# Tower of four Fourier layers: a new order on VectorE in layer 0, and unread TensorE products in layers 0, 1 and 2

## What is computed

```
v = concat(x, gx, gy) @ p_w + p_b                      # one pixel value and two grid values lifted to 32 channels
for i in range(4):
    x_ft = rfft2(v)
    out1 = einsum('bixy,ioxy->boxy', x_ft[:, :, :12, :12],  W1[i])
    out2 = einsum('bixy,ioxy->boxy', x_ft[:, :, -12:, :12], W2[i])
    x1 = irfft2(place out1 and out2 in zeros)
    v = x1 + einsum('bcxy,cd->bdxy', v, w_w[i]) + w_b[i]
    v = batchnorm(v) ; if i < 3: v = relu(v)
out = einsum('bcxy,cu->bxyu', v, q_w) + q_b
```

## Time and profile before

| | |
|---|---|
| median of 3 runs | 760.6 us (759.24, 760.6, 770.03) |
| profiled execution | 765.84 us, span 763.9 us |
| PE busy | 630.4 us, 83% of the span, 10483 instructions |
| DVE busy | 543.5 us, 71% |
| ACT busy | 365.9 us, 48% |
| POOL busy | 51.2 us, 7% |
| mean granted clock of TensorE | 0.933 |
| layer 0 up to the end of mixing | 0 to 41.8 us |
| layer 1, forward transforms and mixing | 125.1 to 204.9 us |
| layer 2, forward transforms and mixing | 286.3 to 369.3 us |
| tower | up to about 577 us of 763.9 |

### The profile page before, as it was taken

The page is one execution under the profiler, slowest core; times in us unless marked ns, Lnnn a source line. Parts: engine busy times, 40 slices in busy tenths (PEclk is TensorE's granted clock), DMA queues, the critical chain, the costliest instruction groups (busy, mean ns, idle before and its releaser), DMA issues. The chain is left out here.

```text
span 763.9 us, 22872 instructions
## 1 busy us (share of the span) xinstructions
PE 630.4 (83%) x10483; PEld 417.0 (55%) x10483; DVE 543.5 (71%) x756; ACT 365.9 (48%) x533; POOL 51.2 (7%) x88
## 2 busy tenths in 40 slices
PE   3799964677799917777999849998998999999997
PEld 2777741234676612336767513344546787887744
DVE  6858886997479878984499858883613867657463
ACT  0015468800045659300155559754403777786762
POOL 4000000002000000001000000001001011111200
PEclk9999996999799969997599959999998999999999
DMA  8101100004012000013011000013104000000001
GB/s 329 27 22 44 44 2 1 1 1 147 3 44 60 6 1 1 1 43 106 6 60 44 2 1 2 2 43 106 30 3 155 2 2 2 1 2 2 1 1 28
DMA packets 11694, 26.31 MB, mean 34 GB/s; under 512 B 3408, under 2 KB 4176, under 8 KB 11600
## 3 DMA queue, kind: packets, MB, share of 16 engines
q1 hardware_dynamic: 11312, 24.21, 9.6%
q10 hardware_dynamic: 288, 0.66, 0.3%
HBM read 24.34 MB, written 0.52 MB: 33 GB/s over the span
## 5 line engine op out<-in xcount | busy, mean ns | idle before, releaser
L459 ACT ACTIVATE V<-ps,wts 128x1024 f32<-128x1024 f32 x96 | 101.8, 1111 | 241.9 <-PE ps L812 241.9
L633 DVE BATCH_NORM_STATS2 stats<-V 128x6 f32<-128x512 f32 x192 | 117.9, 676 | 16.1 <-ACT V L459 16.1
L509 DVE STREAM_TRANSPOSE room<-V 128x2048 f32<-128x2048 f32 x48 | 107.2, 2271 | 6.7 <-ACT V L408 6.7
L705 PE MATMUL ps<-room,tab 128*128 128x384 f32 x192 | 73.9, 523 | 31.1 <-DVE room L516 31.1
L408 ACT ACTIVATE V<-V,small 128x2048 f32<-128x2048 f32 x48 | 96.7, 2085 | 3.8 <-DVE small L660 3.8
L693 PE MATMUL ps<-room,tab 32*32 32x512 f32 x1536 | 67.6, 649 | 24.0 <-DVE room L509 24.0
L705 PEld LDWEIGHTS ps<-room,tab 128*128 128x128 f32 x192 | 35.3, 197 | 80.3 <-DVE room L516 57.3
L812 PEld LDWEIGHTS ps<-tab,room 64*128 64x128 f32 x1024 | 61.3, 192 | 29.6 <-issue 25.2
L627 DVE STREAM_TRANSPOSE room<-ps 128x2048 f32<-128x2048 f32 x24 | 55.6, 2317 | 22.0 <-PE ps L755 22.0
L516 DVE STREAM_TRANSPOSE room<-ps 128x1024 f32<-128x1024 f32 x48 | 56.6, 1217 | 19.4 <-PE ps L693 19.4
L812 PE MATMUL ps<-tab,room 64*128 64x128 f32 x1024 | 67.5, 283 | 1.8 <-DVE room L627 1.8
(11 more groups left out here) (230 smaller groups left out, 887.9 us busy)
## 6 DMA issues: line engine op xcount, KB each, us to landing
room<-in_modes SPq DMA_DIRECT2D x28, 384.0 KB, 5.8
r_ky<-in_modes SPq DMA_DIRECT2D x20, 384.0 KB, 3.1
wl<-in_layers SPq DMA_DIRECT2D x3, 452.0 KB, 5.8
wm<-in_mixture SPq DMA_DIRECT2D x1, 874.5 KB, 8.4
tab<-in_table SPq DMA_DIRECT2D x1, 656.5 KB, 4.8
room<-in_turned SPq DMA_DIRECT2D x1, 512.0 KB, 3.7
V<-in_pixels SPq DMA_DIRECT2D x4, 128.0 KB
out_dram<-ke SPq DMA_DIRECT2D x4, 128.0 KB, 2.5
```

Of the source, the lines that this page charges most:

```text
L459: nc.scalar.activation(Vm[:, 2 * h:2 * h + 2, r, 512 * q:512 * (q + 1)], bank(half_of_u(q, r) + 2 * h, 2).rearrange("p (m n) -> p m n", m= ...
L509: nc.vector.transpose(T[n % 3].rearrange("p (k n) -> p k n", k=16), Vk[:, :, P * n:P * (n + 1)]).then_inc(s_T, 1)
L633: last = nc.vector.bn_stats(stats[:, 16 * q + 4 * r + m, :], Vm[:, m, r, 512 * q:512 * (q + 1)])
L705: last = nc.tensor.matmul(bank(4 + (2 * (u % 2) if l < L - 1 else 0) + pair)[:, 0:MODES * CH], fwd_x[layout][ri], y[:, :, MODES * ri:MODES ...
```

## The change

Three edits. First, in layer 0 VectorE lifts two pairs ahead of the loop instead of three, and in the loop turns pair `k` before it lifts pair `k + 2`, where it lifted pair `k + 3` before it turned pair `k`. Second, TensorE gets unread products in layer 0: two of 512 columns ahead of mixing 0, and two of 256 columns behind each of the six mixing steps (behind the matmul that signals `s_mix`), into columns 256 to 511 of bank 7. Third, in layers 1 and 2 TensorE waits for the first relu of the layer and then issues three unread products of 512 columns ahead of the first `forward_y`. No transfer is added or moved.

```diff
--- before.py
+++ after.py
@@ -609,15 +609,15 @@
                     break
 
                 if l == 0:
-                    for k in range(3):
+                    for k in range(2):
                         lifted(k)
                 for k in range(KYP):
-                    if l == 0 and k + 3 < KYP:
-                        lifted(k + 3)
                     dve.wait_ge(s_mix, KYP * l + k + 1)
                     src = bank(2 * (k % 2), 2).rearrange("p (h j b) -> p b h j", h=2, b=BATCH)
                     dst = MZ[:, 1024 * k:1024 * (k + 1)].rearrange("p (b h j) -> p b h j", h=2, j=16)
                     nc.vector.transpose(dst, src).then_inc(s_Z, 1)
+                    if l == 0 and k + 2 < KYP:
+                        lifted(k + 2)
 
                 def spread_x(quad):
 
@@ -724,6 +724,10 @@
                     if l == L - 1:
                         for m in range(early):
                             convolve(m)
+                    else:
+                        pe.wait_ge(s_relu, PAIRS * (l - 1) + 1)
+                        for _ in range(3):
+                            nc.tensor.matmul(bank(7), first, tab[:, 0:512], start=True, stop=True)
                     forward_y(0)
                     for u in range(FU):
                         between = squares_in(u) if l == L - 1 else ()
@@ -740,6 +744,8 @@
                     pe.wait_ge(s_S, FU * l)
                 else:
                     pe.wait_ge(s_lyt, 2)
+                    for _ in range(2):
+                        nc.tensor.matmul(bank(7), first, tab[:, 0:512], start=True, stop=True)
 
                 def grid_of(quad):
 
@@ -779,6 +785,10 @@
                                 out = bank(2 * (k % 2) + kxh)[64 * par:64 * (par + 1), BATCH * kx:BATCH * (kx + 1)]
                                 last = nc.tensor.matmul(out.rearrange("p (i b) -> p i b", b=2),
                                                         W[ky][rows, kx, :], src, start=True, stop=True, tile_position=(64 * kxh, 64 * par))
+                    if l == 0:
+
+                        for _ in range(2):
+                            nc.tensor.matmul(bank(7)[:, 256:512], first, tab[:, 0:256], start=True, stop=True)
                     if l == L - 1:
 
                         convolve(late + k)
```

## The result

The changed kernel takes 752.5 us in the median of 20 runs (747.4 to 760.8), the kernel before 765.1 in 20 runs beside them (759.2 to 770.5). The ratio is 0.984, with a 95% interval from 0.982 to 0.987: 12 us, or 1.6%, faster, which is within the 2% that the prediction allowed on either side. The median of 760.6 that the prediction started from was that of three runs and turned out 4.5 us too low. So 752 predicted against 752.5 measured is partly luck: two errors cancel, a base 4.5 us too low and a gain of 8.6 us where this comparison shows 10 to 14. Two later comparisons of the same pair gave 0.989 (0.984 to 0.994) and 0.984 (0.980 to 0.987).

A forecast was written before the change was run, and what follows sets the result against it. It saw TensorE at 1.2 GHz in layer 0's mixing and VectorE setting the pace in layer 1's forward transforms. Gains of 6.0 us (layer 0) and 2.6 us (layers 1 and 2) off the 760.6 us median gave 752 us, range 747 to 761.5.

The forecast's parts named there:

- Layer 0: Layer 0: 4.0 us from mixing, 1.8 and 0.5 behind it; taken as 6.0 us, bounds -1.9 and 6.3.
- the rise in the first unread products: Layer 0: TensorE's clock rises between 15 and 20 us and stays up.
- rounds of 3.73 us: Layer 0: one turn and lift on VectorE takes 3.73 us and sets the pace of mixing.
- unread products hidden in TensorE's slack: Layer 0 mixing: a warm TensorE round of 2.9 us fits in VectorE's 3.73, with 0.8 us to spare.
- the last layer's row: Last layer: mixing sharing 3.65 us rounds with other products shows clock 1.00, taken as evidence that layer 0 stays warm.
- the cold order alone: Layer 0: with mixing still at 1.2 GHz, the new order gains 2.5 us if nothing else stands in line.
- Rival A: Layer 0: clock does not rise or hold, unread products queue; rounds 5.2 us, total 763.3 us; chance 0.13.
- second HAM failure mode: TensorE: brief idling between matmul groups lets the clock swing; by this rule Rival A would hold, at 763.3 us.
- The starts: Start of layers 1 and 2: three unread products speed the first y product; 1.3 us each, 2.6 together.
- The bound of 0.4 us for their delay: Start of layers 1 and 2: the three products, if cold, delay the first y product by at most 0.4 us.
- Rival B: Layer 0: warm mixing is not paced by its matmuls (1.28 us stall mid-block); rounds 4.4 us, total 755.4; chance 0.17.
- rival C: Layers 1 and 2: mid-layer clock falls shift, winning or losing 4 to 5 us (747.5 or 756.5); chance 0.10.

The follow-up runs named there:

- e1: The changed kernel without the three unread products at the start of layers 1 and 2; ratio to the kernel before 0.996 (0.993 to 0.999).
- e7: The changed kernel without the pairs of 256-column products behind layer 0's six mixing steps; ratio to the kernel before 0.990 (0.987 to 0.993).
- e4: The kernel before plus only layer 0's unread products, with the old order of lifts and turns; ratio to before 1.001 (0.996 to 1.006).
- e3: The kernel before plus only layer 0's new order of lifts and turns, no new unread products; ratio to before 1.002 (0.997 to 1.007).
- e5: The changed kernel plus two 256-column unread products behind each mixing step of layers 1 and 2; ratio to the kernel before 0.985 (0.982 to 0.988).
- e10: As e5, with four unread products at the norm instead of three at the first relu; ratio to the kernel before 0.984 (0.980 to 0.988).
- e12: Repeat of e1, on another chip; ratio to the kernel before 0.990 (0.986 to 0.994).
- e2: The kernel before plus only the three unread products at the start of layers 1 and 2; ratio to before 0.997 (0.993 to 1.001).
- e13: Repeat of e2; ratio to the kernel before 0.996 (0.992 to 0.999).

## Why the prediction was right, and where not

**Layer 0: the right mechanism, a size near its upper end.** The prediction took 6.0 us; the first pair of traces gives 5.8 at the first L459 (45.24 for 51.05). Each step came out: the rise in the first unread products, rounds of 3.73 us, 1.6 us per 96 records, unread products hidden in TensorE's slack. Over all traces that have the full edits in layer 0 and those that have none, layer 0 ends between 106.6 and 108.8, and between 111.2 and 113.0 us: 4.9 us in the mean, and 4.6 at the first L459. Two things make it less than 6. In three further traces without the edits the clock rises at 46.1 to 46.2 us, not at 51. And the rise between 15 and 20 us does not always last: in four of the seven traces with the edits the clock falls again behind the mixing, between 42 and 49 us, for 3.4 us (6.8 in e1). That the mixing itself stays warm rested on the last layer's row, and e7 shows that it needed the pairs of products.

**What it did not say:** order and products need each other. I had priced the cold order alone at 2.5 us of gain and had not priced the products without the order. The wait of 3.8 us in e4 is the difference. The order is worth 2.1 us by itself in e3's trace, and more than that as the condition under which the products keep the clock up.

**Rival A** was put as a case in which the clock fails by itself. It exists in e4's trace, at the price worked out for a round (5.2 us, 5.45 measured), and in none of the seven traces that also have the new order.

**The Trainium skill's second HAM failure mode** (TensorE: Matmul & The Clock Gate; HAM is its name for what gates TensorE's clock), by which short idle times between groups let the clock swing: e7 agrees, with the clock falling during a wait of 2.14 us after two warm steps. With two 256-column products a step, and waits of 1.07 and three times 0.65 us left, the whole change shows 1.00.

**The starts: the right size, with a wide spread.** 1.3 us a layer was taken. From the norm's aggregate to the first spectra transpose it is 16.46 us in the mean of 12 layers without the products and 15.23 in 14 layers with them (0.5 to 1.7 us less): 1.2 us. In the first trace it was only 0.6 and 0.5 us, since in layer 1 the clock rose at 120.8 us, 6.1 us behind the start of the products, where 3 to 5 had been taken. The bound of 0.4 us for their delay was too small there: 0.8 us.

**Rival B: not in layer 0.** No block of layer 0's mixing stops for 0.3 us or more without a semaphore, in any of the seven traces; warm mixing there is paced by VectorE. In layers 1 and 2 the stops of rival B are real, and they come back below.

**The sum was too small**, 8.6 us for 12.0 (10.3 to 13.7), 8.6 and 12.6 in the three comparisons. By the means above layer 0 and the starts are worth 4.9 + 2.4 = 7.3 us, so some 1 to 5 us lie elsewhere. They lie in rival C, which I had called luck of both signs. In one place it is not luck of the single run: layer 2's mixing took 15.0, 15.2 and 14.7 us in three traces of the whole change and 19.9 and 20.2 in two of the kernel before; layer 1's took 18.0, 19.0, 18.8 and 18.3, 15.9. With layer 0 alone it was 21.8 and 20.4 in layer 2, in e3 and e4 20.4 and 21.4, without the holding products 21.1. In layer 2's mixing, TensorE first stops for an "issue" gap of 0.86 us in the changed kernel and 1.38 in the one before:

```profile
345.83 0.24 PE L786 MATMUL ps<-MZ,room 64*64 64x32 f32 x1 [0.86 <-issue]
```

```profile
353.38 0.78 PE L780 MATMUL ps<-MZ,r_ky 64*64 64x32 f32 x37 [1.38 <-issue]
```

The other six traces with a slow layer 2 (19.9 us or more) have gaps of 1.36 to 2.54 us; these two are e1 and e7:

```profile
345.80 0.97 PE L782 MATMUL ps<-MZ,r_ky 64*64 64x32 f32 x28 [2.54 <-issue]
```

```profile
347.07 1.17 PE L786 MATMUL ps<-MZ,r_ky 64*64 64x32 f32 x37 [2.02 <-issue]
```

In all seven the clock falls 0.03 to 1.4 us behind the end of that gap. The kernel before, busy time, clock and transfers (share and GB/s, the last two columns) by microsecond around it:

```profile
350.00:351.00 1.00, 1.00 (x84) 1.00 (x78) 0.00 (x0) 0.00 (x0) 0.00 (x0) 1.00 0.98 372
351.00:352.00 1.00, 1.00 (x67) 0.89 (x59) 0.85 (x1) 0.00 (x0) 0.59 (x1) 1.00 0.38 145
352.00:353.00 1.00, 0.00 (x0) 0.00 (x0) 0.40 (x1) 0.00 (x0) 0.59 (x1) 1.00 0.06 25
353.00:354.00 1.00, 0.62 (x37) 0.62 (x37) 0.00 (x0) 0.00 (x0) 0.59 (x1) 1.00 0.00 0
```

**What the gaps are.** The traces answer this when TensorE's matmul records are counted from the start of the program. In the twelve that have such gaps in the mixing of layers 1 and 2, whatever products had been added, they stand only behind record 2511, 2639, 2766, 2894 or 3021, and behind 4928 (or 4929), 5056, 5183 or 5310: 127 or 128 records apart, as many weight loads between them. Behind each of the 56 gaps of 0.25 us or more TensorE goes on 1.2 to 1.6 us after a packet of 16384 bytes on the instruction queue has ended; in the kernel before that packet runs from 351.16 to 352.09 us and the gap ends at 353.38. So they are waits for instructions, at places fixed in the stream. The later the packet starts behind the place before, the longer the gap: 1.38 us for a start 1.24 us behind it in the kernel before, where the 16 engines have only just come down from full load with mixing weights, and 2.54 for 2.26 in e1. Warm, 127 records of small products take about 2.1 us (1.60 for 96), while the time from one such place to the next is 3.0 us or more wherever there is a gap. The Trainium skill's Runtime: NRT & Kernel Launch, Instruction fetch mechanics, calls the crossing of a block mostly hidden; by these gaps of 0.3 to 2.9 us it is not hidden in a warm stream of 64x32 products. With the holding products of e5 and e10 in the stream there is no gap at all.

**What the change does to them.** It puts 40 matmul records (and 40 weight loads) ahead of layer 2's mixing, so the mixing begins behind record 4814 and not 4774. Before, record 4929 lies 155 records into the mixing, and the whole stretch from 4802 on is small products. With the whole change it lies 115 in, and the stretch begins in the slower forward products: no gap there in three traces, and none of the clock's falls. Without part of the products the place comes back inside: 127 records in for e1, e12 and e4, 138 for e7, each with a long gap and a fall. e7 is the nearest thing to a test, as it has the text of the changed kernel in layers 1 and 2 and 24 records fewer ahead of them.

That the gap is what makes the clock fall is argued, not shown: e2 and e13 have gaps of 1.47 and 1.17 us there (142 records in), and the clock stays up for another 13 us in one and through the mixing in the other. No run shifted the stream by instructions that do nothing else. Nor do the timed runs single this term out: the whole against its halves left an excess of 1.5 us, well within its error. So of the 12 us, some 7 come from the two mechanisms of the prediction. The term that it had too small is rival C, put at 4 to 5 us of either sign with a chance of 0.10: the traces put 5 us of gain there, in layer 2's mixing, likely by the place of the instruction blocks, and that cause stays open.

## What to carry to other kernels

An unread product that keeps TensorE's clock up is worth its place only where TensorE has slack once it is warm, and is pure cost where the clock fails; so shorten the waits first, then add the products, and test both together, since each alone may show nothing. An added instruction also shifts every later one against the blocks in which the stream is fetched; where a stage is made of many short products, count the records to see where its stops will stand. Put the products behind the matmul that signals, and look at the duration of like instructions rather than at the clock column for the true level. A change of a per cent may move the clock somewhere else by more than it gains, so cut the trace by stages before the total is explained.

## What the runs showed of the hardware

- The column of the granted clock reads 1.00 from the start of every trace up to its first change, also where the mixing of layer 0 runs at half speed (2.78 us per 96 records in the kernel before, 1.60 with the change).
- 64x64 products with 32 columns do not hold the clock safely: in the seven traces with a gap of 1.36 to 2.54 us in the first steps of layer 2's mixing, and no holding products there, it fell right behind the gap. They can keep it: with shorter gaps it stayed at 1.00 through that mixing in three traces of the changed kernel and in e13. Two 128x128 products of 256 columns a step went with 1.00 in all twelve steps of e5 and of e10.
- In layer 0 the clock stayed up over waits of 1.07 us between steps with such products (seven traces) and fell in waits of 3.80 us with them (e4) and 2.14 us without them (e7), one trace each.
- A product of 128x128 by 512 columns costs 0.86 us warm and 1.71 cold, in 32-bit floating point: 0.43 and 0.85 us from record to record.
- In a warm block of small products TensorE stops for 0.3 to 2.9 us with no semaphore to wait for, at the same records of the stream in every kernel (every 127 or 128), and goes on 1.2 to 1.6 us after a 16384-byte packet of instructions has ended.
